# Small operations of finished panels moved to GpSimd, and one late unit in eight summed on TensorE

## The reference

```
# layer 0: inverse degree times (alpha*adj + (1-alpha) on the diagonal) @ x, @ W.T + b, relu
x = layernorm(x + relu(...))
# layer 1
x_tangent = x * artanh(norm(x)) / norm(x)
par = adj   * sigmoid(s_left_par[:, None] + s_right_par[None, :])
chi = adj.T * sigmoid(s_left_chi[:, None] + s_right_chi[None, :])
support = chi @ x_tangent + par @ x_tangent
y = tanh(norm(support)) * support / norm(support), scaled down where its norm is over 1 - 1e-5
out = layernorm(x + y)
```

## Time and profile before

| what | value |
|---|---|
| median of 3 runs | 2293.18 us |
| the profiled execution, its time | 2295.63 us |
| its span in the profile | 2293.8 us |
| busy share PE, DVE, ACT, POOL | 88%, 89%, 58%, 58% |
| bytes moved by DMA | 818.28 MB, mean 357 GB/s |
| mean granted TensorE clock | 0.965 |

### The profile page before, as it was taken

One profiled execution on the slowest core, in us unless ns is written; L12 is line 12 of the kernel. 1 busy time (PEld: TensorE's weight loads), 2 busy tenths in 40 slices (PEclk: granted clock), 3 DMA queues, 4 the chain that ended last, 5 costly groups with the idle time before them and its releaser, 6 DMA issues.

```text
span 2293.8 us, 18436 instructions
## 1 busy us (share of the span) xinstructions
PE 2020.7 (88%) x5100; PEld 896.8 (39%) x5100; DVE 2034.3 (89%) x1945; ACT 1335.3 (58%) x1512; POOL 1321.7 (58%) x543
## 2 busy tenths in 40 slices
PE   8999999999999989999989778887797787778776
PEld 3444444444444434434434323332242233224224
DVE  5676868988999988989988888999999999999996
ACT  0011224443554464454354787978888888888896
POOL 0000206335455455444444777988788887978895
PEclk9999999999999999999999888999899999999998
DMA  9988889889899889888888998999889989997992
GB/s 329 353 329 309 361 300 393 352 346 378 358 377 420 349 346 384 372 342 353 365 333 350 421 378 333 374 400 410 347 342 399 409 321 385 387 360 327 377 415 84
DMA packets 129206, 818.28 MB, mean 357 GB/s; under 512 B 14912, under 2 KB 27456, under 8 KB 33360
## 3 DMA queue, kind: packets, MB, share of 16 engines
q1 hardware_dynamic: 122304, 796.97, 87.4%
q10 hardware_dynamic: 6800, 20.13, 2.3%
HBM read 808.59 MB, written 8.45 MB: 356 GB/s over the span
## 4 chain that ended last, share of the span: by engine, by line
PE 36%; DVE 21%; issue 15%; POOL 15%; ACT 9%; DMA 3%; DVEq 0%; ACTq 0%; SPq 0%; POOLq 0%
PE ps L1075 24%; POOL chi L528 11%; PE ps L1144 9%; DVE ps L924 8%; DVE dsum L828 5%; ACT chi L660 3%; DMA ring<-in_g_blk 3%; POOL xA L528 3%; DVE keys L931 2%; ACT ps L677 2%; PE ps L1154 2%; ACT L660 1%; POOL acc L537 1%; DVE dsum L824 1%; DVE fs L953 1%
## 5 line engine op out<-in xcount | busy, mean ns | idle before, releaser
L528 POOL TENSOR_TENSOR chi<-chi,ring 128x1024 f32<-128x1024 f32 x323 | 826.1, 2570 | 717.2 <-ACT chi L660 657.1
L1144 PE MATMUL ps<-keys,xtA 128*128 128x512 f32 x2048 | 1023.9, 631 | 216.1 <-DVE keys L931 188.0
L1075 PE MATMUL ps<-ring,xA 128*128 128x512 f32 x2048 | 921.5, 600 | 38.3 <-DMA ring<-in_g_blk 34.2
L677 ACT ACTIVATE ps<-scores,prcr 128x1024 f32<-128x1024 f32 x472 | 524.1, 1110 | 475.7 <-DVE keys L931 456.2
L1144 PEld LDWEIGHTS ps<-keys,xtA 128*128 128x128 f32 x2048 | 383.7, 199 | 789.9 <-issue 751.6
L828 DVE TENSOR_TENSOR dsum<-dsum,ring 128x2048 f32<-128x2048 f32 x240 | 592.6, 2469 | 38.1 <-DMA ring<-in_g_blk 31.2
L1075 PEld LDWEIGHTS ps<-ring,xA 128*128 128x128 f32 x2048 | 389.1, 192 | 530.3 <-issue 482.4
L931 DVE TENSOR_TENSOR keys<-ps,chi 128x1024 f32<-128x1024 f32 x430 | 526.5, 1224 | 55.3 <-issue 26.2
L924 DVE TENSOR_TENSOR ps<-ps,ring 128x1024 f32<-128x1024 f32 x410 | 501.1, 1222 | 68.3 <-ACT ps L677 65.5
L660 ACT ACTIVATE chi<-scores,prcr 128x1024 f32<-128x1024 f32 x430 | 488.2, 1135 | 14.4 <-DMA scores<-plcl_d 6.9
L528 POOL TENSOR_TENSOR chi<-chi,xA 128x1024 f32<-128x1024 f32 x107 | 251.8, 2367 | 50.7 <-ACT chi L660 49.5
(11 more groups left out here) (104 smaller groups left out, 778.9 us busy)
## 6 DMA issues: line engine op xcount, KB each, us to landing
ring<-in_g_blk SPq DMA_DIRECT2D x461, 1024.0 KB, 8.9
ring<-in_a_cols SPq DMA_DIRECT2D x186, 1024.0 KB, 8.4
xA<-in_a_cols SPq DMA_DIRECT2D x70, 1024.0 KB, 9.2
xA<-in_g_blk SPq DMA_DIRECT2D x31, 1024.0 KB, 8.7
scores<-plcl_d ACTq DMA_DIRECT2D x22, 512.0 KB, 8.4
xA<-in_x_g SPq DMA_DIRECT2D x64, 64.0 KB, 13.0
yb<-in_xT ACTq DMA_DIRECT2D x8, 512.0 KB, 8.8
x_d<-res ACTq DMA_DIRECT2D x8, 512.0 KB, 9.1
```

What stands on the lines that cost most here:

```text
L528: pool.tensor_tensor(out=chi(n), in0=chi(n), in1=half(t, n), op=ALU.mult).then_inc(m2_ready, 1)
L677: act.activation(dst, scores[:, row, 0, :], ACT.Sigmoid, bias=prcr[:, 2 * jt:2 * jt + 1]).then_inc(p_ready, 1)
L1075: ins = pe.matmul(Y[:, h * BANK:(h + 1) * BANK], xA[:, tile * D:(tile + 1) * D], t[:, tt * BP + h * BANK:tt * BP + (h + 1) * BANK], start= ...
L1144: ins = pe.matmul(outp[:, h * BANK:(h + 1) * BANK], xtA[:, jt * D:(jt + 1) * D], keys(n)[:, h * BANK:(h + 1) * BANK], start=begins, stop=i ...
```

## The change

1. Of the eight steps of `factor_step` the two reciprocals stay on VectorE (`norm_inverse`); the other six go to GpSimd, as `norm_floor` (one operation), `mapped_norm` (three) and `scales` (two). `final_shift`, one operation with two steps, becomes two operations on GpSimd (`shift`). All are called in GpSimd's unit loop ahead of `second_product(n)`. The steps get new places: the chain's middle at step 13 instead of 11 to 13, the second reciprocal at 14, the scales at 16, and slot, residual, statistics and variances two steps later; ScalarE's normalising begins at 14 instead of 13.
2. In the units of `APART` (n = 194, 202, ... with n mod 8 = 2, own units left out: 35 units) VectorE writes its product straight into `keys(n)` and adds nothing. TensorE adds `xtA.T @ keys(n)` and `xtA.T @ chi(n)`, four matmuls instead of two, and `chi(n)` is free when kt_used says so. `SUMS[n]` is the count of k_ready up to unit n.

```diff
+APART = {n for n in range(MORE + 8, UNITS) if n % 8 == 2 and n not in OWN_AT}
+SUMS = [n + 1 - sum(m in APART for m in range(n + 1)) for n in range(UNITS)]
...
-            if kind == "unit":
-                eng.wait_ge(k_ready, i + 1)
+            if kind == "unit" and i in APART:
+                eng.wait_ge(m1_ready, i + 1)
+            elif kind == "unit":
+                eng.wait_ge(k_ready, SUMS[i])
...
+            def norm_floor(k):
+                at = slice(k * TPP, (k + 1) * TPP)
+                pool.wait_ge(f_norm, k + 1)
+                pool.tensor_scalar(s_nm[:, at], s_n[:, at], MIN_NORM, None, ALU.max).then_inc(f_step, 1)
+            def mapped_norm(k):
+                at = slice(k * TPP, (k + 1) * TPP)
+                pool.wait_ge(f_step, f_steps(k, 2))
+                pool.wait_ge(f_tanh, k + 1)
+                pool.tensor_tensor(out=s_s1[:, at], in0=s_th[:, at], in1=s_rn[:, at], op=ALU.mult).then_inc(f_step, 1)
+                pool.wait_ge(f_step, f_steps(k, 3))
+                pool.tensor_tensor(out=s_n2[:, at], in0=s_s1[:, at], in1=s_n[:, at], op=ALU.mult).then_inc(f_step, 1)
+                pool.wait_ge(f_step, f_steps(k, 4))
+                pool.tensor_scalar(s_n2[:, at], s_n2[:, at], MIN_NORM, None, ALU.max).then_inc(f_step, 1)
+            def scales(k):
+                at = slice(k * TPP, (k + 1) * TPP)
+                pool.wait_ge(f_step, f_steps(k, 6))
+                pool.tensor_scalar(s_s[:, at], s_s[:, at], MAXNORM, 1.0, ALU.mult, ALU.min).then_inc(f_step, 1)
+                pool.wait_ge(f_step, f_steps(k, 7))
+                pool.tensor_tensor(out=s_s[:, at], in0=s_s1[:, at], in1=s_s[:, at], op=ALU.mult).then_inc(f_step, 1)
+            def shift(k):
+                at = slice(k * TPP, (k + 1) * TPP)
+                pool.wait_ge(rs_ready, k + 1)
+                pool.tensor_tensor(out=s_mb[:, at], in0=mvf[:, at, 0], in1=s_rs[:, at], op=ALU.mult).then_inc(mb_raw, 1)
+                pool.wait_ge(mb_raw, k + 1)
+                pool.tensor_scalar(s_mb[:, at], s_mb[:, at], -1.0, None, ALU.mult).then_inc(bias_ready, 1)
...
+                for k, (_, b) in enumerate(FINALS):
+                    final(k, n - b)
                 second_product(n)
...
-                if before is not None:
-                    act.wait_ge(k_ready, before + 1)
+                if before in APART:
+                    act.wait_ge(kt_used, before + 1)
+                elif before is not None:
+                    act.wait_ge(k_ready, SUMS[before])
...
-                dve.tensor_tensor(out=s, in0=s, in1=other, op=ALU.mult).then_inc(m1_ready, 1)
+                if n in APART:
+                    dve.wait_ge(kt_used, n - KB + 1)
+                dve.tensor_tensor(out=keys(n) if n in APART else s, in0=s, in1=other, op=ALU.mult).then_inc(m1_ready, 1)
             def key(n):
+                if n in APART:
+                    return
...
-                pe.wait_ge(k_ready, n + 1)
+                if n in APART:
+                    pe.wait_ge(m1_ready, n + 1)
+                else:
+                    pe.wait_ge(k_ready, SUMS[n])
                 for h in range(BP // BANK):
                     ins = pe.matmul(... keys(n) ...)
+                if n in APART:
+                    pe.wait_ge(m2_ready, n + 1)
+                    for h in range(BP // BANK):
+                        ins = pe.matmul(... chi(n) ..., start=False, stop=is_end(n))
                 ins.then_inc(kt_used, 1)
```

More of the change, by code:

```diff
@@ L125 @@
 FIN_OF = {p: k for k, (p, _) in enumerate(FINALS)}
-F_EVAC, F_SQUARE, F_NORMS, F_NORMS_SLOT, F_ROOT, F_FLOOR, F_INV, F_RSTD, F_TANH, F_CHAIN, F_NORM, F_TURN, F_SLOT, \
-    F_ADD, F_STATS, F_AGGR = 3, 4, 4, 6, 7, 8, 9, 9, 12, 11, 13, 14, 16, 17, 18, 26
+F_EVAC, F_SQUARE, F_NORMS, F_NORMS_SLOT, F_ROOT, F_FLOOR, F_INV, F_RSTD, F_SHIFT, F_TANH, F_MAPPED, F_INV2, F_SCALES, \
+    F_NORM, F_TURN, F_SLOT, F_ADD, F_STATS, F_AGGR = 3, 4, 4, 6, 7, 8, 9, 9, 11, 12, 13, 14, 16, 14, 16, 18, 19, 20, 28
 F_LOADX = 16
 F_STORE = 36
-L_ROOT, L_RSTD, L_NORM = 34, 36, 38
+L_ROOT, L_RSTD, L_SHIFT, L_NORM = 34, 36, 37, 40
 F_STEPS = 8
@@ L419, in adj_resnorm_kernel @@
         rs_ready = sem("rs_ready")
+        mb_raw = sem("mb_raw")
         bias_ready = sem("bias_ready")
@@ L537, in add_taken, with final @@
                 pool.tensor_tensor(out=at, in0=taken[:, :], in1=at, op=ALU.add).then_inc(acc_added, 1)
+            def norm_floor(k):
[23 more added lines that the diff above has]
+                pool.tensor_scalar(s_mb[:, at], s_mb[:, at], -1.0, None, ALU.mult).then_inc(bias_ready, 1)
+            def final(k, i):
+                if i == F_FLOOR:
+                    norm_floor(k)
+                if i == F_MAPPED:
+                    mapped_norm(k)
+                if i == F_SCALES:
+                    scales(k)
+                if k > 0 and i == F_SHIFT:
+                    shift(k - 1)
+                if k == NPAN - 2 and i == L_SHIFT:
+                    shift(k)
             for g in range(PAIRS):
@@ L552, in _ @@
                     add_taken(EVAC_AT_UNIT[n])
+            k = NPAN - 1
+            norm_floor(k)
+            mapped_norm(k)
+            scales(k)
+            shift(k)
         @block.scalar
@@ L932, in key, with norm_inverse @@
                                   op=ALU.add).then_inc(k_ready, 1)
-            def factor_step(k, i):
+            def norm_inverse(k, i):
                 at = slice(k * TPP, (k + 1) * TPP)
-                if i == 0:
-                    dve.wait_ge(f_norm, k + 1)
-                else:
[L941 to L960, removed]
+                dve.wait_ge(f_step, f_steps(k, i))
+                if i == 1:
+                    dve.reciprocal(s_rn[:, at], s_nm[:, at]).then_inc(f_step, 1)
+                else:
+                    dve.reciprocal(s_s[:, at], s_n2[:, at]).then_inc(f_step, 1)
             def add_residual(k):
@@ L989, in final_inverse @@
                 dve.reciprocal(s_rs[:, at], s_sd[:, at]).then_inc(rs_ready, 1)
[L991 to L995, removed]
             def final(k, i):
-                if i == F_FLOOR:
-                    factor_step(k, 0)
                 if i == F_INV:
-                    factor_step(k, 1)
-                if F_CHAIN <= i < F_CHAIN + F_STEPS - 2:
-                    factor_step(k, i - F_CHAIN + 2)
+                    norm_inverse(k, 1)
+                if i == F_INV2:
+                    norm_inverse(k, 5)
                 if k > 0 and i == F_RSTD:
                     final_inverse(k - 1)
-                if k > 0 and i == F_RSTD + 1:
-                    final_shift(k - 1)
                 if i == F_ADD:
@@ L1016, in final @@
                         final_inverse(k)
-                    if i == L_RSTD + 1:
-                        final_shift(k)
             def constants():
@@ L1051, in _ @@
             k = NPAN - 1
-            for i in range(F_STEPS):
-                factor_step(k, i)
+            norm_inverse(k, 1)
+            norm_inverse(k, 5)
             add_residual(k)
@@ L1141, in products @@
                 pe.wait_ge(xt_ready, jt // TPP + 1)
-                pe.wait_ge(k_ready, n + 1)
+                if n in APART:
+                    pe.wait_ge(m1_ready, n + 1)
+                else:
+                    pe.wait_ge(k_ready, SUMS[n])
                 for h in range(BP // BANK):
                     ins = pe.matmul(outp[:, h * BANK:(h + 1) * BANK], xtA[:, jt * D:(jt + 1) * D],
-                                    keys(n)[:, h * BANK:(h + 1) * BANK], start=begins, stop=is_end(n))
+                                    keys(n)[:, h * BANK:(h + 1) * BANK], start=begins,
+                                    stop=is_end(n) and n not in APART)
+                if n in APART:
+                    pe.wait_ge(m2_ready, n + 1)
+                    for h in range(BP // BANK):
+                        ins = pe.matmul(outp[:, h * BANK:(h + 1) * BANK], xtA[:, jt * D:(jt + 1) * D],
+                                        chi(n)[:, h * BANK:(h + 1) * BANK], start=False, stop=is_end(n))
                 ins.then_inc(kt_used, 1)
```

## The result

The changed kernel takes 2235.1 us (median of four runs, 2233.74 to 2237.35) against 2294.44 us: ratio 0.9743, 95% interval 0.9726 to 0.9760. Taken again beside later experiments it was 0.9733 (0.9718 to 0.9747). The forecast was 2246 us. The profiled executions differ by 58.3 us of span (2293.8 to 2235.5).

The account below looks back on a forecast made before the run. VectorE, 97% busy in the late part, was taken as the bound. Gains of 38.4 (three cycles), 8.0 behind, 2 before and -1 in the tail, 47.4 us, took 2295.6 to 2248.2, less 2.4 to 2246 us; range 2218 to 2274.

Parts of the forecast that it names:

- its small operations are waits for GpSimd: VectorE's small finish operations stand until GpSimd's product is over; moving them removes 17.4 us per cycle of 72 units.
- Moved operations cost 0.3 us on GpSimd: Each finish's 8 operations on GpSimd cost 0.3 us apiece with handoff, 4.8 us per cycle.
- rival (d): GpSimd's small operations are dear: at 2.35 us each the cycle is 206 us, the time 2307; chance 0.02.
- The later places change no sum: Moving residual and statistics two units later shifts 5.7 us of work per finish and changes no sum.
- Units apart lift 9.6 us per cycle off VectorE and free `chi` 2.9 us later, hidden: Eight additions per cycle leave VectorE at 1.20 us each; the later chi release is covered while ScalarE and GpSimd are free.
- 174.8 us of work: VectorE's work per cycle after the change: 201.8 less 17.4 and 9.6 us, so it stops being the bound.
- Sum of block bounds 183: Cycle after the change, adding each block's largest load of any engine: 183 us.
- DMA makes it 189: Keeping all 9.6 us of DMA idle time in the own block lengthens the cycle to 189 us.
- the branch that I had put at 183 to 185: Cycle of 183 to 185 us if the DMA engines first work off a backlog in the own block.
- Before unit 230: 2 us: Four additions leave VectorE before the three cycles; blocks limited by GpSimd at 18.6 instead of 19.18 us gain 2 us.
- rival (b): DMA binds at once and the own block's idle time stays: cycle 197 us, time 2275; chance 0.20.
- rival (a): All freed time is gained: cycle 177 to 180 us, 85 us saved, time 2208; chance 0.13.

Follow-up runs that it names:

- e1: The changed kernel with no units apart, so only the small operations moved to GpSimd: 2245.7 us, 0.9776 of the kernel before.
- e8: The kernel before with its finish steps at the changed kernel's later places, all operations still on VectorE: 2268.5 us, 0.9878 of the kernel before.
- e10: The changed kernel with no units apart and normalising, turn, slot, residual, statistics and variances at their old places: 2248.6 us, 0.9794 of the kernel before.
- e5: The changed kernel with the load ring cut from 7 to 6 and one more chi and keys buffer each: 2279.3 us, 0.9933 of the kernel before.
- e6: The changed kernel with the load ring cut from 7 to 6 and nothing else: 2279.8 us, 0.9924 of the kernel before.
- e3: The changed kernel with late adj loads cut to 768 of 1024 columns: 2231.9 us, 0.9724 of the kernel before.

## Why the forecast held, point by point

- *VectorE is the one full engine, and its small operations are waits for GpSimd.* Right: e1 removes them and gains 51 us.
- *Moved operations cost 0.3 us on GpSimd.* Measured 0.20 to 0.26; rival (d) is dead. In the tail the operations with their handoffs cost 0.9 us more, as forecast; it came out even (25.5 and 25.4 us behind the last first product) since TensorE's squared norms took 2.20 instead of 3.19 us.
- *The later places change no sum.* Wrong, and no term of mine carried it: with the operations on VectorE they are worth 28 us (e8). It did not spoil the sum, since after the move only about 1 us of it is left (e10). I had read how long the operations stood and not asked whether they had to stand at that place.
- *Units apart lift 9.6 us per cycle off VectorE and free `chi` 2.9 us later, hidden.* Right where it was tried, with a ring of six (e5 against e6), and VectorE's busy time per cycle fell by 25.6 us where 27.0 were forecast. Its "174.8 us of work" was a cycle's length with 6.3 us of idle time in it; the work left is 170.0. Right as well was the block behind the own ones, 20.1 us forecast and 19.91 measured, where a unit apart costs.
- *Sum of block bounds 183, DMA makes it 189.* The first is the measured mechanism: 185.2, with the chain blocks too low by up to 2.5 us (23.48 for 21.0, 22.41 for 21.5) and the plain block too high (17.91 for 18.6: GpSimd works off a lead that it won in the blocks before). The second was the term that failed: I kept 9.6 us of idle DMA time in the own block; measured 3.6 (0.19 x 19.17), as a backlog was worked off there, the branch that I had put at 183 to 185. And e3 says more: with a quarter of the bytes gone the cycle is still 184.6 us, so loads did not set it, and this term had no place in the sum of that cycle; what set it were the engines' loads block by block. That the forecast was near is in part luck: with 183 in place of 189 the same sum gives, as an estimate, 2224 us, 11 too low, as it is 11 too high with 189. A cycle gained 16.6 and not 12.8 us, 61% of the 27.0 freed; three cycles 48.4 instead of 38.4, and the part behind 9.8 instead of 8.0.
- *Before unit 230: 2 us.* 1.5 us, hidden in the span by a layer 0 that happened to take 1.5 us longer. Two blocks of eight units (206 to 222) fall from 19.18 to 18.70 and 18.61, as forecast; the unit apart at 202 costs its block 0.35 us instead.
- *Readings.* "Four resources within 15%" of VectorE holds for three: TensorE, 677.1 of 821.1 us, is 18% below. And the eight records of 5.40 us in the earlier trace rows were at half clock for part of the time only: the granted clock of that stretch is 0.68. Neither is in the sum.
- *Signs.* VectorE at 92% (715.1 of 780 us), DMA at 0.98 and 402 GB/s: as written. Waits for loads at own units only, 2.8 us in all, so rival (b) fell (e3); rival (a) would have needed a cycle of 177 to 180, below the sum of the block bounds.

## What to carry to other kernels

A small operation that shows ten times its free duration is a wait; look at what runs beside it at its start, and try another place for it as well as another engine; here the place brought half of what the engine did. When the fullest engine is relieved, sum the others block by block: the gain ends there or before, and each further relief pays only in blocks that the engine still bounds. Two parts that each shorten the same waits don't add up either: list what each of them changes before blaming a shared limit. A DMA share of 1.01 did not show a bound here; cutting the bytes did show where there was one.

## What was not expected of the hardware

Here GpSimd did a 128 x 8 operation in 0.20 us (two inputs) or 0.24 to 0.26 (one input and constants), against VectorE's 0.16 to 0.17 with GpSimd idle: little difference at this size, where at 128 x 1024 GpSimd took 2.36 us. And VectorE's products out of or into PSUM, 1.22 us each, kept their length beside a running GpSimd product, before and after (1.21 to 1.23 us over all 318 first products of the late part behind 1400 us), while the small operations stood.
